# Moving one mask, one D half, one fp16 split and the carry order in a hand-scheduled Mamba-style scan kernel

## What is computed

```python
xr, gate = split(x @ W_in.T);  xr = xr + t_emb[:, None, :]
xc = silu(causal_conv4(xr) + b_conv)
xn = layernorm(xc) * ln_g + ln_b
Bm, Cm, dt = split(xn @ W_xproj.T, 3)
Ad = 1 - 0.01 * tanh(dt @ W_dt.T + b_dt) * tanh(A_log)
Bd = Bm * min(norm(xn), 1)
h  = clip(h * Ad[:, None] + Bd[:, None] * xn_t[None, :], -10, 10)   # step by step
y  = einsum(C_t, h) + D * xn
out = x + (y * silu(gate)) @ W_out.T
```

## Time and profile before

| | before |
|---|---|
| median of 3 runs | 2055.43 us (2054.57 to 2057.09) |
| profiled execution | 2052.24 us, its span 2050.5 us |
| busy share | PE 89%, POOL 86%, DVE 80%, ACT 67% |
| period of one chunk in the middle | 61.24 us |

### The profile page before, as it was taken

The page is one execution under the profiler, slowest core; times in us unless marked ns, Lnnn a source line. Parts: engine busy times, 40 slices in busy tenths (PEclk is TensorE's granted clock), DMA queues, the critical chain, the costliest instruction groups (busy, mean ns, idle before and its releaser), DMA issues.

```text
span 2050.5 us, 46002 instructions
## 1 busy us (share of the span) xinstructions
PE 1826.6 (89%) x16240; PEld 1396.0 (68%) x16240; DVE 1637.6 (80%) x2109; ACT 1376.2 (67%) x3462; POOL 1753.4 (86%) x1476
## 2 busy tenths in 40 slices
PE   5689998899999899999898999899999899899888
PEld 4466776676776676676676777676677676677655
DVE  3478887888887888888887888788888788888786
ACT  5577666777666776766676766676766677766643
POOL 1489988889988889988889988889988889988886
PEclk9799999999999999999999999999999999999999
DMA  5222222222222222222222222222222222222221
GB/s 178 58 69 54 70 58 74 63 78 59 67 58 75 62 79 59 67 57 77 62 77 59 67 63 71 62 75 59 69 72 62 64 73 61 67 75 58 62 67 29
DMA packets 168069, 139.14 MB, mean 68 GB/s; under 512 B 100704, under 2 KB 137968, under 8 KB 163168
## 3 DMA queue, kind: packets, MB, share of 16 engines
q1 hardware_dynamic: 167840, 136.20, 24.9%
HBM read 62.07 MB, written 9.31 MB: 35 GB/s over the span
## 4 chain that ended last, share of the span: by engine, by line
PE 29%; POOL 25%; issue 19%; ACT 15%; DVE 8%; SPq 2%; DMA 1%; POOLq 0%; DVEq 0%; ACTq 0%
POOL prod L1094 17%; PE ps_y L590 6%; ACT tap L750 5%; PE ps_job L517 5%; PE ps_job L483 4%; DVE ks L995 4%; PE ps_fill L573 3%; PE ps_fill L564 3%; ACT low L793 3%; PE ps_job L496 2%; POOL xn L1039 2%; POOL xn L1042 2%; PE ps_job L490 2%; SPq L406 1%; ACT xh L688 1%
## 5 line engine op out<-in xcount | busy, mean ns | idle before, releaser
L1094 POOL TENSOR_TENSOR prod<-ks,crep 128x512 f32<-128x512 f32 x1024 | 1286.0, 1274 | 142.1 <-DVE ks L995 140.4
L995 DVE TENSOR_TENSOR_SCAN ks<-low,ps_fill 128x512 f32<-128x512 f32 x1024 | 1208.3, 1208 | 227.0 <-PE ps_fill L573 226.7
L793 ACT COPY low<-ps_fill 128x512 f32<-128x512 f32 x1024 | 584.6, 580 | 477.0 <-PE ps_fill L564 474.4
L590 PE MATMUL ps_y<-c_sb,prod 128*128 128x128 f32 x4096 | 613.4, 275 | 9.9 <-ACT xc L758 7.1
L590 PEld LDWEIGHTS ps_y<-c_sb,prod 128*128 128x128 f32 x4096 | 457.5, 142 | 75.9 <-issue 27.1
L573 PE MATMUL ps_fill<-spans,pick 128*128 128x512 f16 x1024 | 390.7, 381 | 76.4 <-ACT low L793 71.8
L564 PEld LDWEIGHTS ps_fill<-ts,xs 128*128 128x128 f16 x4096 | 315.8, 98 | 171.8 <-issue 10.7
L564 PE MATMUL ps_fill<-ts,xs 128*128 128x128 f16 x4096 | 397.9, 220 | 9.2 <-DMA xs<-h 7.6
L750 ACT ACTIVATE tap<-xr,cols_sb 128x128 f32<-128x128 f32 x768 | 251.9, 393 | 0.0
L478 PE MATMUL ps_job<-x,w_in 128*128 128x128 f16 x3072 | 215.9, 221 | 10.3 <-POOL x L1064 7.8
L483 PE MATMUL ps_job<-w_in,x 128*128 128x512 f16 x768 | 202.0, 379 | 21.3 <-ACT gate L682 21.3
(11 more groups left out here) (124 smaller groups left out, 1962.7 us busy)
## 6 DMA issues: line engine op xcount, KB each, us to landing
crep<-c_dram SPq DMA_DIRECT2D x32, 1024.0 KB, 4.7
xs<-xh SPq DMA_DIRECT2D x256, 64.0 KB, 2.0
xs<-xl SPq DMA_DIRECT2D x224, 64.0 KB, 2.0
xf<-in_xT SPq DMA_DIRECT2D x32, 256.0 KB, 2.8
res<-in_x SPq DMA_DIRECT2D x32, 256.0 KB, 2.8
out_dram<-res SPq DMA_DIRECT2D x32, 256.0 KB, 2.3
ts<-tth SPq DMA_DIRECT2D x128, 32.0 KB
ts<-tth SPq DMA_DIRECT2D x128, 31.0 KB
```

The lines of the kernel that those rows point to most:

```text
L590: last = mm(ps_y[:, cut], prod[:, (TILES * k + s) % HOLD, e, :], ident, start=False, stop=(u % 4 == 3 and q == 3 and e == QN - 1), is_tran ...
L793: copy(low[:, (TILES * k + s) % RING], ps_fill[:, (TILES * k + s) % RING]).then_inc(sem["low_copied"], 1)
L995: nc.vector.tensor_tensor_scan(ks[:, u % 2, QN * q:QN * (q + 1)].rearrange("d n t -> d (n t)"), low[:, g % RING], ps_fill[:, g % RING], 0. ...
L1094: tt(prod[:, g % HOLD], ks[:, u % 2, part], crep[:, p, part], ALU.mult).then_inc(sem["weighed"], 1)
```

## The change

Five things change. (1) POOL makes the second half of D*xn at tile 22, no longer at tile 11 with the first, and the second mask `ttl` at tile 21, no longer at 18. (2) The fp16 remainder of x (`x16[:, p, 1]`) is made by DVE at point 15 and no longer by POOL at tile 6. (3) ACT's copy to `lend` moves one point later, waits for DVE's carry remainder, and DVE no longer waits for it; the PSUM bank of a carry half counts as free when `lend` is made. (4) ACT's half of `bqm` moves from point 27 to 29, and the taps move. (5) The second gate job starts at point 9, and ACT reads it at 13.

```diff
-                (7, 1, "yT", 1, -1, 2, 1), (8, 4, "gate", 1, 0, 2, 0),
+                (7, 1, "yT", 1, -1, 2, 1), (9, 4, "gate", 1, 0, 2, 0),
-        TAKE = {("z", 0): 5, ("gate", 0): 7, ("hend", 0): 6, ("yT", 1): 8, ("gate", 1): 12,
+        TAKE = {("z", 0): 5, ("gate", 0): 7, ("hend", 0): 6, ("yT", 1): 8, ("gate", 1): 13,
-        TAP_AT = [24, 28, 30, 34, 38, 40, 43, 46]
+        TAP_AT = [24, 28, 33, 38, 40, 42, 44, 47]
...
-                    pe.wait_ge(sem[name + "_taken"], (kk + off) * per + i + 1)
+                    freed = "lend_set" if name == "carry" else name + "_taken"
+                    pe.wait_ge(sem[freed], (kk + off) * per + i + 1)
...
                     copy(ch[:, half], bank("carry", i)).then_inc(sem["carry16"], 1)
+                for i in range(2):
+                    if point != TAKE["carry", i] + 1 or not exists(k, 1):
+                        continue
+                    half = slice(i * BANK, (i + 1) * BANK)
+                    act.wait_ge(sem["carry_taken"], 2 * (k + 1) + i + 1)
                     if exists(k, 0):
                         act.wait_ge(sem[f"lend_in{p}"], 16 * pair(k, p, 0))
                     copy(lend[:, half], bank("carry", i)[0:NS]).then_inc(sem["lend_set"], 1)
-                if point == 27 and exists(k, 1):
+                if point == 29 and exists(k, 1):
...
+                if point == 15 and exists(k, 2):
+                    dve.wait_ge(sem["xT_high"], k + 3)
+                    tt(x16[:, p, 1], xf[:], x16[:, p, 0], ALU.subtract).then_inc(sem["xT_low"], 1)
...
-                    dve.wait_ge(sem["lend_set"], 2 * j + i + 1)
                     stt(cc[:, half], ch[:, half], neg_low, bank("carry", i), ALU.mult, ALU.add
...
+                        skipped(p, 0)
+                    if s == 22 and exists(k, 0):
                         since(pool, "yT_in1", N_YT * k)
-                        for i in range(2):
-                            half = slice(i * BANK, (i + 1) * BANK)
-                            tt(xd[i], xn[:, p, half], row_d[:, half], ALU.mult).then_inc(sem["xd_done"], 1)
+                        skipped(p, 1)
...
-                    if s == 6 and exists(k, 2):
-                        pool.wait_ge(sem["xT_high"], k + 3)
-                        tt(x16[:, p, 1], xf[:], x16[:, p, 0], ALU.subtract).then_inc(sem["xT_low"], 1)
...
-                    if s in (14, 18) and exists(k, 1):
-                        h = s // 4 - 3
+                    if s in (14, 21) and exists(k, 1):
+                        h = s // 21
```

More of the change, by code:

```diff
@@ L1078, in body, with skipped @@
                            ALU.mult).then_inc(sem["tt_done"], 1)
+            def skipped(p, i):
+                half = slice(i * BANK, (i + 1) * BANK)
+                tt(xd[i], xn[:, p, half], row_d[:, half], ALU.mult).then_inc(sem["xd_done"], 1)
             def carrier(p):
```

## The result

The changed kernel takes 2136.77 us (median of 4 runs, 2127.58 to 2144.61) against 2055.0 us of before (2051.99 to 2057.09): 1.0397 times as long, 95% interval 1.0348 to 1.0447. The profiled execution has 2131.83 us with a span of 2130.0.

The account below looks back on a forecast made before the run. No engine was full, so a chain through several engines was taken as the bound. 2.5 us at 29 boundaries (72.5) plus 9 at the two ends gave +81.5 on the median 2055.43: 2137 us, range 2110 to 2160 (chance 0.75).

Parts of the forecast that it names:

- The 2.0 us to spare: At the tile-0 fill of a middle chunk: the DMA chain had 17.59 - 15.6 = 2.0 us of room.
- 15.6 us from the first mask DMA to the fill: Time from SP's first mask DMA to the next chunk's tile-0 fill when nothing else decides, read at chunks 0 and 30.
- Scan 21 to SP in 3.6 us: From DVE's scan 21 through POOL's product and mask to SP's first DMA: 1.29 + 1.25 + 1.03 + 0.03 us.
- The carry: Ahead of tile 21: the reordered ACT, DVE and PE carry work brings scan 21 0.7 us earlier.
- PE's wait at the carry job: New wait of PE's carry matmuls for ACT's `bqm`, put at 1.75 us.
- PE's own lateness behind ACT: PE behind ACT's copy of the convolution: 0.8 us longer to the next first fill, hidden as the stack is later.
- the stack: Work ahead of the tile-0 fill: both masks, 12 mask DMAs, `lend`, three carry rows, two state rows.
- the count of ACT's steps behind tile 21: ACT's `lend`, four fill copies, gated copy and three tap sets from 1049.95, ending its convolution copy near 1058.6.
- The DVE remainder of x: The fp16 remainder on DVE, put at 1.7 us (0.67 plus 1.03 waiting for POOL) and hidden by DVE's waits.
- the rival I gave 0.08: DVE's remainder hits POOL's 2.24 us instruction in each chunk, uncovered: 31 x 0.9 us on top, 2165; chance 0.08.
- The gate, "nothing": Gate job one point later, behind tile 7's widen, tile 8's widen staying where it was: no cost or gain.
- The sum: First fill 2.5 us later at 29 chunk boundaries, 4.5 at the first and last: +81.5 us, 2137 us.

Follow-up runs that it names:

- b_mask21: Kernel before with one edit, the second mask at tile 21 instead of 18: 2186.7 us, ratio 1.0639.
- b_mask20: Kernel before with one edit, the second mask at tile 20 instead of 18: 2072.4 us, ratio 1.0092.
- b_carry: Kernel before with the order of `lend`, the bank rule, `bqm` at point 29 and the new tap points: 2069.3 us, ratio 1.0075.
- a_mask18: Changed kernel with one thing undone, the second mask back at tile 18: 2071.4 us, ratio 1.0085 to before.
- b_carry27: Kernel before with the order of `lend`, the bank rule and the new tap points, `bqm` left at point 27: 2053.0 us, ratio 0.9998.
- b_x16: Kernel before with only the low fp16 half of x moved from POOL to DVE: 2060.7 us, ratio 1.0036.

## Why the prediction was right

It gave 2137 us; measured were 2136.8. Point by point:

*The 2.0 us to spare, and 15.6 us from the first mask DMA to the fill.* Right. The distance in the middle of the changed kernel is 15.5 in the median (15.35 to 15.71, once 16.32), and 15.72 in the chunk shown of b_mask21; a delay of 2.5 us (b_mask20) costs 0.43 a period and one of 5.2 (b_mask21) 3.8 and more, the clock's part in it.

*Scan 21 to SP in 3.6 us.* Right in both kernels (3.60).

*The carry.* Direction right, size a little low: scan 21 comes 1.1 us earlier in the loop and not 0.7, of which 0.24 is the gate's, not the carry's. PE's wait at the carry job was put at 1.75 and is 1.56. PE's own lateness behind ACT was put at 0.8 a period; the carry edits alone make it 0.58 (b_carry). With the stack out of the way (a_mask18) it is 0.68, which is what the single runs add up to: 0.58 and 0.33 of `x` less 0.24 of the gate. The carry's part comes from `bqm`'s place, as b_carry27 shows, and not from the count of ACT's steps behind tile 21 that I gave.

*The DVE remainder of x.* Put at 1.7 us and hidden. It took 0.7 in most chunks of the change, and 1.65 in the median of a_mask18; in b_x16 it took 1.4 and cost 0.33 us a period. So in the kernel before it was not hidden in full, nor did it cost its full length. In the change five chunks met POOL's long instruction, the rival I gave 0.08; they are the five periods of 66.

*The gate, "nothing".* Wrong: -0.24 a period. I had read that tile 8's `widen` does not move, but the weights of the `zT` job just behind it wait 0.28 us for ACT's `z`, and that wait did go.

*The sum.* The 29 middle periods of the trace together rose by 72.6 us, where the sum had 72.5, but not in the way it said. In 24 of them the rise is 2.0 us on average (1.9 to 2.2 but for two, of 1.1 and 2.8) and not 2.5, 12 us less. The other five rose by 4.9, which makes 12 us more, and for these the sum has no term. At the two ends 4.5 us each were put in, and 5.2 and 2.3 came. At the end of chunk 30 the first mask DMA had started 0.44 us behind scan 21 already, so that the mask came only 3.15 later there and not 5.2. The median's agreement within 1 us is therefore partly luck. The run-to-run spread, 17 us against 5 of before, would fit a varying number of such chunks; that was not tested.

These long periods have two parts. In the chunk from 281.42, PE's second gate job starts 14.28 us after the first fill, in the one from 218.09 12.62. The windows of the kernel after, the same stretch behind the first fill of each of the two chunks:

```profile
218.10:220.70 2.60, 2.23 (x22) 1.94 (x23) 2.00 (x3) 2.19 (x5) 2.60 (x3) 1.00 0.68 210
220.70:224.70 4.00, 4.00 (x39) 3.32 (x38) 3.44 (x3) 2.84 (x6) 3.34 (x3) 1.00 0.24 65
281.40:284.00 2.60, 2.21 (x18) 1.96 (x19) 1.90 (x3) 2.16 (x5) 2.55 (x3) 0.85 0.64 203
284.00:288.00 4.00, 4.00 (x30) 3.26 (x29) 2.30 (x2) 2.31 (x4) 3.27 (x2) 0.67 0.27 69
```

The first part, 1.66 us, is PE at a lower granted clock (0.67 in these 4 us) behind the stall of 1.58. It shifts PE and DVE by more than POOL, DVE's instruction falls on POOL's long one, PE waits 1.07 us for its result, and the fill behind that is 1.24 later again. I read the granted clock of the first 3.5 us behind the fill, and the duration of DVE's instruction, in the 28 chunks from 218.09 to 2004.92: in the five long ones the clock is 0.75 or 0.76 and the instruction lasts 2549 to 2556 ns, in the other 23 the clock is 1.00 and the instruction lasts 694 to 754. That the clock brings about the meeting, and not only goes with it, is read from their order in time; no run took one away and left the other. What makes the clock fall behind some stalls of 1.3 to 1.7 us and not behind others of the same length, nor behind the one of 2.32 in these chunks, stays open.

## What to carry to other kernels

Before moving an instruction that many engines have slack for, ask which queue starts only behind it: here twelve DMA issues of 0.6 us turned a mask that nobody needed for 17 us into the bound, and sending those that don't need it first made the move free. Chunks at the ends, where a chain already binds, show its length, and the difference to the middle ones is the slack; a delay costs only what goes beyond it. Here a stall of PE of some 3 us was paid again in clock.

## What the runs showed of the hardware that I had not expected

Behind stalls of some 3 us (b_mask21) PE's granted clock was 0.50 to 0.62 over the next 3.5 us in each of the 20 middle chunks that I read, and down to 0.72 in the 4.5 us behind these in every fourth or so; it cost 0.6 to 2.6 us a period more than the stall. In the changed kernel it fell behind five of 27 stalls of 1.3 to 1.7 us, and not behind one of 2.32. A DVE tensor_tensor with both inputs in SBUF that started 0.13 us after a POOL instruction of 2.14 us lasted 2.56 instead of 0.7, and each such instruction ended 0.55 us after the POOL instruction that it met; POOL's next one lasted 0.45 longer.
